# A graph layer with gathered rows: single-row loads issued from a second queue, another setup order and another tail

## The chip, the cores and the metric

One core of a Trainium2 chip. The metric is device time in microseconds, the median of several runs of the whole program. The profile is one execution of it, recorded by the hardware profiler.

## The reference

One message-passing layer over 12500 nodes and 400000 edges (the edges come sorted by destination), then a residual and a layer norm:

```python
h_s = s @ lin1_ws * a * _inv(S_IN)                       # per node: 64 scalars
h_v = jnp.einsum('nci,cd->ndi', v, lin1_wv) * a ...      # and 32 vectors of 3
hid = jax.nn.silu(edge_scalars @ fc_w1 * _inv(R))        # per edge: 64 -> 64
w = hid @ fc_w2 * _inv(FC_HID)                           # 64 -> 224 weights
es, ev = h_s[edge_src], h_v[edge_src]                    # gather, 160 floats an edge
...                                                      # products of w, es, ev and edge_attr
agg = segment_sum(mid, edge_dst)                         # back to nodes
out = gate(sc(x) + lin2(agg))                            # per node
x = _layernorm(x + out)
```

## The kernel before

**Setup.** A first block turns the node features into the table `h_table` (12500 rows of 160 floats) in memory, 4 x 128 nodes at a time, and prepares weights and index columns. SyncE's queue brings its inputs in program order, beginning with `lin1_ws` and `lin1_wv`; ScalarE's queue stores the table; VectorE builds the padded weights and the checks of the index pattern between its shares of the table.

**Tiles, quads, rounds.** The edges are 3128 tiles of 128; four tiles are a quad (782), eight quads a round (97 rounds and a rest of 6 quads). Edge tile t needs the 128 rows of `h_table` that its sources name, in one slot of the ring `rows` (16 quads deep).

**Who brings the rows.** GpSimd issues one indirect DMA per tile (`gather`, L961), in the order of the tiles. A quad's gathers wait until an earlier quad has been summed (`freed`, L965: after the first 96 quads, the quad two before). The first 8 quads are made in setup. For the quads in `FETCHED` the fourth tile is left out of GpSimd's list (`gathered`, L52): SyncE brings it, as 128 DMAs of one row each (`fetch`, L863), whose addresses it loads into registers eight at a time (L866). A tile is spread over `TRIP` = 3 rounds, then handed over by one DMA into the ring slot (`hand_over`, L871). There are 30 such tiles.

**A quad's work.** VectorE: one-hot selection, seven products of weights and rows (`all_products`, L757 to L768), the window pattern. TensorE, in order: the next quad's edge weights (`weights`, L1320), every second quad the hidden layer (`hidden`, L1312), the sums of the quad before (`combine`, L1339 and L1341), the sums of this quad's tiles (`sum_tiles`, L1328). ScalarE, in order: every second quad the hidden activation (`activate`, L1012, and the load of the next edge features, L996), the copy of the combined sums (`copy_out`, L1022, four instructions), the copy of the tile sums (`copy_tiles`, L1046), the store of the quad before (`store`, L1041), which waits until the copied sums are complete and until the store before it has landed. Once a round ScalarE loads the round's eight window bases into registers (`load_bases`, L1029).

**Nodes.** Each round finishes one block of 128 nodes: SyncE loads its sums and inputs once the first quad of a later round is stored (`node_begin`, L846), TensorE turns them (L1349, L1355) and multiplies (`node_lin`, L1364), ScalarE applies the gates (L1061 to L1063) and the square root (L1067), VectorE adds and normalises, SyncE stores (`node_store`, L828). SyncE's program runs a round as: node loads, first part of its rows, the store, second part of its rows. The last two blocks have buffers of their own (`spare`) in the ring's memory and are done behind the last quad, with `keep_warm` multiplications ahead of each (L1367).

All engines run their programs in order and meet at semaphores. The loops of rounds on TensorE, ScalarE, VectorE and GpSimd are written out; SyncE's is a loop.

Of the kernel before, what the change touches and what calls it, by code (L numbers as in the profile page):

```python
# [12 lines left out]
ds = bass.ds  # L13
# [27 lines left out]
TRIP = 3  # L41
# [3 lines left out]
def fetched_quad(k):  # L45
    return RING * (TRIP * k + 7) + RING - 1


FETCHED = [fetched_quad(k) for k in range(2 * TRIPS)]


def gathered(q):  # L52
# [107 lines left out]
def setup_block(nc, io, m):  # L160

    with ExitStack() as ctx:
# [109 lines left out]
        def _(sp):  # L272

            sp.dma_start(stage_s[:], io["lin1_ws"]).then_inc(s_lin1, 16)
            for i in range(K4):
                sp.dma_start(l1v[V * i:V * i + V, :], io["lin1_wv"]).then_inc(s_lin1, 16)

# [15 lines left out]
            for c in range(1, HCHUNKS):  # L293
                load_x(c, CB * P)
                if c == 5:
                    load_dst(0)
                if c == 7:
                    load_dst(1)
                if c == 9:
# [34 lines left out]
        def _(dve):  # L334
# [48 lines left out]
            def clear():  # L383
                nc.vector.memset(m.fc2[:], 0.0)
                nc.vector.memset(m.fc1[:], 0.0).then_inc(s_fc, 1)
                nc.vector.memset(m.w5[:], 0.0)
                then(nc.vector.memset(m.mscv[:], 0.0))
# [14 lines left out]
            def self_weights():  # L402
                dve.wait_ge(s_w, n_w)
                nc.vector.tensor_scalar(m.mscs[:], stage_sc[:], S ** -0.5, None, ALU.mult)
# [64 lines left out]
            for n, (kind, c) in enumerate(UNITS):  # L469
# [17 lines left out]
                if n == 6:  # L487
                    self_weights()
                    lin2_weights(0)
                if n == 7:  # L490
                    lin2_weights(1)
                    lin2_weights(2)
                if n == 8:
                    lin2_weights(3)
                    local_nodes(0)
                for k in range(4):
                    if k and n == 8 + 3 * k:
                        local_nodes(k)
                    if n == 9 + 3 * k:
                        extreme(2 * k, m.local[:, quarter(k)], ALU.max)  # L500
                    if n == 10 + 3 * k:
                        extreme(2 * k + 1, m.local[:, quarter(k)], ALU.min)
                if n == 20:
                    window_starts()
                if n == 21:
                    earlier_starts()
                if n == 22:
                    window_steps()
                if n == 23:
                    quad_reach()  # L510
                if n == 24:
                    extreme(8, m.off[:, 0, :], ALU.max)
                    extreme(9, m.off[:, 0, :], ALU.min)
                if n == 25:
                    extreme(10, delta, ALU.max)
                    extreme(11, delta, ALU.min)
                if n == 26:
                    orders()
                if n == 27:
# [71 lines left out]
        def _(act):  # L591
            act.dma_start(m.src[:, 0:SRC_FIRST], io["srcT"][:, 0:SRC_FIRST]).then_inc(s_src, 16)
# [46 lines left out]
def edge_block(nc, io, m):  # L639

    with ExitStack() as ctx:
# [11 lines left out]
        fidx = sb("fetch_indices", [1, P], I32)  # L653
        sel = sb("sel", [P, PRING, QT, K4, W8])
# [44 lines left out]
        fetch_idx = sem("fetch_indices_loaded")  # L699
        handed = [sem(f"handed_over{b}") for b in range(2)]  # L700
        fetch_rows = [sem(f"fetched_rows{b}") for b in range(2)]
# [10 lines left out]
        n_in = [sem(f"n_in{c}") for c in range(3)]  # L712
        n_turned = sem("n_turned")
# [81 lines left out]
        def spare_bufs(v):  # L795
# [9 lines left out]
            return psum_bufs(o, bank[:, 0:512], bank[:, 512:512 + P], bank[:, 512 + P:512 + P + 2 * SO])  # L805
# [4 lines left out]
        def _(sp):  # L810
# [6 lines left out]
            def node_inputs(k, width, bufs, c):  # L817
                nodes, r = ds(k * P, width), slice(0, width)
                sp.dma_start(bufs.xin, io["xN"][ds(k * P, P), :]).then_inc(n_in[c], 16)

            def node_load(k, width, bufs, c, free):
# [4 lines left out]
                node_inputs(k, width, bufs, c)  # L826
# [6 lines left out]
            def round_of(R, quads, loading, storing):  # L833
                node_begin(R, loading, storing)
                if quads < RING:
                    sp.wait_ge(prod_ready, SPARE_FREE)
                    sp.sem_inc(loads_seen, 1)
                    node_inputs(NBLK - 2, P, spare[0], 1)
                    node_inputs(NBLK - 1, LASTN, spare[1], 2)
# [23 lines left out]
            def fetch(b, first, last):  # L863

                for at in range(first, last, BATCH):
                    sp.load(places, fidx[0:1, at:at + BATCH])  # L866
                    for n in range(BATCH):
                        node = sp.snap(places[n], min_val=0, max_val=N - 1)
                        sp.dma_start(fetched[b][at + n:at + n + 1, :], m.h[ds(node, 1), :]).then_inc(fetch_rows[b], 16)

            def hand_over(k, b, trip):  # L871

                p = FETCHED[b] % PLACES
                sp.wait_ge(fetch_rows[b], 16 * P * (trip + 1))
                sp.sem_inc(loads_seen, 1)
# [116 lines left out]
        def _(act):  # L992
# [37 lines left out]

            def store(q, i, b, u, free):
# [21 lines left out]
            def node_copy_last(k, width, bufs):  # L1053
                act.wait_ge(n_turned, 2 * k + 2)
                nc.scalar.activation(bufs.turned[:, 4, 0:width], bufs.last[:, 0:width], ACT.Copy).then_inc(n_freed, 1)

# [12 lines left out]
            def round_of(R, quads, first, turning, gating, edges=False):  # L1069
                rest = quads < RING  # L1070
                for u in range(quads):
# [14 lines left out]
                    if rest and u == 5:  # L1086
                        node_gates(R - 2, P, late)
                    if u == 0:
                        load_bases(R, quads)
                    if edges:  # L1090
                        load_edges(u)
                    if gating and u == 6:
                        node_std(R - 3, P, main)

            with act.If(miss == 0):
# [9 lines left out]
                node_copy(NBLK - 2, P, spare[0])  # L1105
                node_copy_last(NBLK - 2, P, spare[0])
                node_gates(NBLK - 2, P, spare[0])
                node_copy(NBLK - 1, LASTN, spare[1])
                node_copy_last(NBLK - 1, LASTN, spare[1])
# [29 lines left out]
        def _(dve):  # L1139
# [9 lines left out]
            def products(I, u, tiles=QT):  # L1149
# [19 lines left out]
                if q in FETCHED:  # L1169
                    dve.wait_ge(handed[FETCHED.index(q) % 2], 16 * (FETCHED.index(q) // 2 + 1))  # L1170
                vec = rows[:, QT * p:QT * p + QT, :]
# [134 lines left out]
        def _(pe):  # L1306
# [51 lines left out]
            def node_lin(k, width, bufs):  # L1358
# [3 lines left out]
                steps += [(outs, bufs.xs[:, 0:width], m.mscs[:]), (outv, bufs.xv[:, 0:width], m.mscv[:])]  # L1362
# [4 lines left out]
            def keep_warm(times):  # L1367

                for n in range(times):
# [164 lines left out]
```

## Time and profile before

| | |
|---|---|
| median of 3 runs | 3951.13 us (3949.48 to 3951.44) |
| the profiled execution | 3948.7 us, span 3946.9 us |
| TensorE busy | 94% of the span |
| GpSimd busy | 74% |
| VectorE busy | 62% |
| ScalarE busy | 51% |
| DMA queues, share of 16 engines | GpSimd's 25.4%, ScalarE's 15.5%, SyncE's 6.5% |
| gathers by GpSimd | 3063 |
| rows by SyncE | 3840 DMAs of 640 bytes |

The busy shares say how much of the span an engine's instructions fill. Issuing a DMA, loading a register and waiting are not in them, so an engine whose program issues many DMAs can be occupied for much longer than its share says. A stretch must be cut at whole rounds if times per round are to be read from it.

### The profile page before, as it was taken

How to read it: one execution, taken by the hardware profiler on the slowest of the kernel's cores; microseconds unless marked ns; L12 is line 12 of the kernel's file. 1: busy time of each engine (PE TensorE's matmuls, PEld its weight loads, DVE VectorE, ACT ScalarE, POOL GpSimd, SP SyncE). 2: the span in 40 equal slices, each digit the busy share in tenths (PEclk: the TensorE clock that was granted, in tenths of full speed). 3: DMA queues.
4: the chain of work that ended last, by engine and by line, in shares of the span. 5: the costliest groups of instructions: out<-in, count | busy, mean ns of one | idle time of the engine just before them, and what ended most of it. 6: DMA issues, size and time to landing. Idle time of an engine off the chain costs nothing.

```text
span 3946.9 us, 76077 instructions
## 1 busy us (share of the span) xinstructions
PE 3705.6 (94%) x18692; PEld 1564.4 (40%) x18692; DVE 2440.5 (62%) x7711; ACT 2023.7 (51%) x5186; POOL 2936.1 (74%) x3119
## 2 busy tenths in 40 slices
PE   7999999999999999999999999999999999999998
PEld 5344443433333334333333333333343333333333
DVE  6666666666656666666666666666666666666665
ACT  3455555554545555555555555555555555555554
POOL 5777777777777777777777777777777777777774
PEclk8999999999999999999999999999999999999999
DMA  7644444444444444444444444444444444444443
GB/s 272 181 132 126 135 133 123 129 127 128 125 129 125 129 124 130 125 129 125 129 124 130 124 130 125 130 124 129 125 128 128 127 127 126 128 125 130 125 128 98
DMA packets 378173, 519.98 MB, mean 132 GB/s; under 512 B 71248, under 2 KB 257366, under 8 KB 377562
## 3 DMA queue, kind: packets, MB, share of 16 engines
q0 software_dynamic: 148944, 254.01, 25.4%
q10 hardware_dynamic: 164522, 180.81, 15.5%
q1 hardware_dynamic: 64224, 79.97, 6.5%
q8 instruction: 151, 2.47, 0.3%
q14 instruction: 332, 2.72, 0.2%
HBM read 431.98 MB, written 80.06 MB: 130 GB/s over the span
## 4 chain that ended last, share of the span: by engine, by line
POOL 49%; PE 19%; issue 17%; DMA 7%; DVE 5%; ACT 0%; ACTq 0%; DVEq 0%; SPq 0%
POOL rows L961 49%; PE psw L1320 6%; DMA rows<-h_table,src_cols 6%; PE pst_e L1328 5%; DVE prod L757 4%; PE psg L1341 2%; PE psg L1339 2%; PE psx L1312 2%; DMA agg_table<-aggsb 1%; DVE prod L768 1%; DVE prod L767 1%; PE psx L1364 1%; ACT aggsb L1022 0%; PE psx L1349 0%; PE psw L1364 0%
## 5 line engine op out<-in xcount | busy, mean ns | idle before, releaser
L961 POOL DMA_INDIRECT rows<-h_table,src_cols x3063 | 2895.8, 945 | 966.9 <-issue 933.0
L757 DVE TENSOR_TENSOR prod<-psw,rows 128x384 f32<-128x384 f32 (+2 forms) x3128 | 1213.1, 450 | 1396.8 <-DMA rows<-h_table,src_cols 1059.0
L1320 PE MATMUL psw<-fc,hid 128*128 128x448 f32 x3128 | 1393.3, 568 | 3.0 <-ACT hid L1012 3.0
L1022 ACT ACTIVATE aggsb<-psg 32x160 f32<-32x160 f32 x3128 | 923.4, 295 | 560.0 <-PE psg L1341 519.5
L1339 PE MATMUL psg<-tsum,shifts 128*64 128x320 f32 x3126 | 1008.8, 445 | 1.0 <-ACT tsum L1046 1.0
L1328 PE MATMUL pst_e<-prod,sel 128*32 128x448 f32 x6256 | 751.9, 552 | 199.7 <-DVE prod L768 196.4
L1341 PE MATMUL psg<-tsum,shifts 128*64 128x288 f32 x3126 | 925.7, 419 | 0.0
L1320 PEld LDWEIGHTS psw<-fc,hid 128*128 128x128 f32 x3128 | 533.0, 190 | 872.5 <-issue 861.6
L1339 PEld LDWEIGHTS psg<-tsum,shifts 128*64 128x64 f32 x3126 | 363.4, 136 | 432.2 <-issue 353.4
L1012 ACT ACTIVATE hid<-psx 128x512 f32<-128x512 f32 x391 | 233.8, 598 | 557.3 <-PE psx L1312 532.1
L1046 ACT ACTIVATE tsum<-pst_e 128x448 f32<-128x448 f32 x782 | 425.5, 544 | 147.0 <-PE pst_e L1328 129.6
L1341 PEld LDWEIGHTS psg<-tsum,shifts 128*64 128x64 f32 x3126 | 363.5, 136 | 149.3
L1312 PE MATMUL psx<-es,fc 128*128 128x512 f32 x782 | 401.2, 595 | 6.8 <-DMA es<-in_esP 3.8
L1328 PEld LDWEIGHTS pst_e<-prod,sel 128*32 128x32 f32 x6256 | 123.1, 108 | 607.3 <-DVE prod L768 448.1
L767 DVE TENSOR_TENSOR prod<-psw,rows 128x256 f32<-128x256 f32 x782 | 324.6, 415 | 0.0
L1175 DVE TENSOR_TENSOR shifts<-psd,tile_offset 128x256 f32<-128x256 f32 x782 | 324.5, 415 | 0.0
L768 DVE TENSOR_TENSOR prod<-psw,rows 128x256 f32<-128x256 f32 x782 | 324.5, 415 | 0.0
L1159 DVE TENSOR_TENSOR sel<-psd,e_cols 128x128 f32<-128x128 f32 x782 | 222.1, 284 | 13.4
L1312 PEld LDWEIGHTS psx<-es,fc 128*128 128x128 f32 x782 | 148.5, 190 | 153.9 <-issue 147.2
L1061 ACT ACTIVATE act_s<-psx,a_cols 128x64 f32<-128x64 f32 x95 | 29.9, 314 | 323.7 <-PE psx L1364 310.1
L1364 PEld LDWEIGHTS psx<-w,turned 128*128 128x128 f32 x960 | 161.8, 191 | 36.5 <-issue 36.5
L1012 ACT ACT_TABLE_LOAD x94 | 120.6, 1283 | 105.3 <-PE psw L1320 101.6
(168 smaller groups left out, 1341.8 us busy)
## 6 DMA issues: line engine op xcount, KB each, us to landing
es<-in_esP ACTq DMA_DIRECT2D x391, 256.0 KB
agg_table<-aggsb ACTq DMA_DIRECT2D x782, 80.0 KB
fetched<-h_table SPq DMA_DIRECT2D x3840, 0.6 KB
rows<-h_table,src_cols POOLq DMA_INDIRECT x3063
nag<-agg_table SPq DMA_DIRECT2D x96, 320.0 KB
nxin<-in_xN SPq DMA_DIRECT2D x96, 208.0 KB
h_table<-e_cols ACTq DMA_DIRECT2D x24, 320.0 KB, 6.1
out<-yn SPq DMA_DIRECT2D x95, 80.0 KB
```

Of the source, the lines that this page charges most:

```text
L757: return nc.vector.tensor_tensor(out, w_part, ev, ALU.mult)
L767: nc.vector.tensor_tensor(w2, w[:, :, 0:S].rearrange(halves, c=V), vec[:, :, 0:S].rearrange(halves, c=V), ALU.mult)
L768: return nc.vector.tensor_tensor(out[:, :, V * B1A:V * B1A + S], w[:, :, S + 3 * V:WN], vec[:, :, 0:S], ALU.mult)
L961: nc.gpsimd.indirect_dma_start(out=rows[:, p * QT + j, :], out_offset=None, in_=m.h, in_offset=bass.IndirectOffsetOnAxis(ap=m.src[:, t:t + ...
L1012: nc.scalar.activation(hid[:], psx[:], ACT.Silu, scale=HID ** -0.5).then_inc(hid_ready, 1)
L1022: ins = nc.scalar.activation(aggsb[r, b, :], joined(psg[r, :], k), ACT.Copy)
L1046: nc.scalar.activation(tsum[:, b, 0:PW], pst[:, 0:PW], ACT.Copy).then_inc(tsum_copied, 1)
L1312: nc.tensor.matmul(psx[:], m.fc1[:], es[:], start=True, stop=True).then_inc(hid_summed, 1)
L1320: ins = nc.tensor.matmul(psw[b][:, 2 * c:2 * c + 2, 0:WN], hid[:, at:at + P], m.fc2[:].rearrange("p (t w) -> p t w", t=2)[:, :, 0:WN], sta ...
L1328: ins = nc.tensor.matmul(pst[W * j:W * j + W, 0:PW], sel[:, q % PRING, j, :, :], prod[:, q % PRING, j, :], start=True, stop=True, tile_pos ...
L1339: nc.tensor.matmul(psg[0:2 * W, 0:2 * AW].rearrange("p (s c) -> p s c", s=2), shifts[:, q % PRING, h, 0:2, :], low, start=(h == 0), stop=( ...
L1341: ins = nc.tensor.matmul(psg[2 * W:P, 0:HIGH], shifts[:, q % PRING, h, 2:K4, :], sums[:, 0:HIGH], start=(h == 0), stop=(h == before), tile ...
```

## The change

- `TRIP` becomes 2: SyncE brings a tile in two rounds instead of three, 64 rows in each, 16 addresses to a register load; 46 tiles instead of 30.
- ScalarE brings one tile in four rounds: behind the store of each quad of rounds 3 to 94 it issues four DMAs of one row each, from 32 registers that it loads once a round. The finished tile is handed over by a DMA of its own, in the third quad of the next group's first round, for a quad one round later. 23 tiles.
- GpSimd leaves those tiles out.
- Setup: `lin1_ws` and `lin1_wv` are issued by ScalarE, ahead of its other loads; SyncE loads the destination columns two to three chunks later; VectorE's preparation steps move with them.
- Tail: no `keep_warm`; the third-last block's multiplication and gates move behind the last quad's; a spare block is turned by five transposes and one copy, and the two multiplications with its own inputs come first, into another PSUM bank.

```diff
-TRIP = 3
+TRIP = 2
 def fetched_quad(k):
-    return RING * (TRIP * k + 7) + RING - 1
+    return RING * (TRIP * k + TRIP + 4) + RING - 1
+ACT_ROWS = 4
+ACT_ROUNDS = P // (RING * ACT_ROWS)
+ACT_GROUPS = (ROUNDS - 4) // ACT_ROUNDS
+def act_quad(k):
+    return RING * (ACT_ROUNDS * (k + 1) + 4) + 3
 def gathered(q):
-    return LAST_REAL if q == QUADS - 1 else QT - (q in FETCHED)
-BATCH = 8
-FETCH_ROWS = [(0, 24, 40), (40, 64, 88), (88, 112, P)]
+    return LAST_REAL if q == QUADS - 1 else QT - (q in FETCHED or q in ACT_FETCHED)
+BATCH = 16
+FETCH_ROWS = P // TRIP
...
-            sp.dma_start(stage_s[:], io["lin1_ws"]).then_inc(s_lin1, 16)
-            for i in range(K4):
-                sp.dma_start(l1v[V * i:V * i + V, :], io["lin1_wv"]).then_inc(s_lin1, 16)
...
-                if c == 5:
+                if c == 7:
                     load_dst(0)
-                if c == 7:
+                if c == 10:
                     load_dst(1)
...
+            act.dma_start(stage_s[:], io["lin1_ws"]).then_inc(s_lin1, 16)
+            for i in range(K4):
+                act.dma_start(l1v[V * i:V * i + V, :], io["lin1_wv"]).then_inc(s_lin1, 16)
             act.dma_start(m.src[:, 0:SRC_FIRST], io["srcT"][:, 0:SRC_FIRST]).then_inc(s_src, 16)
...
-                        fetch(b, FETCH_ROWS[r][0], FETCH_ROWS[r][1])
+                        fetch(b, r, 0)
                         node_store(R - 3, P, main)
-                        fetch(b, FETCH_ROWS[r][1], FETCH_ROWS[r][2])
+                        fetch(b, r, 1)
                     hand_over(k, b, trip)
...
+            sources = [act.alloc_register(f"source{n}") for n in range(RING * ACT_ROWS)]
+            def load_indices(k):
+                act.dma_start(act_idx[k % 2][:], io["srcR"][ds(act_quad(k) * QT + QT - 1, 1), :]).then_inc(act_indexed[k % 2], 16)
+            def load_places(k, r):
+                if r == 0:
+                    act.wait_ge(act_indexed[k % 2], 16 * (k // 2 + 1))
...
+                at = RING * ACT_ROWS * r
+                act.load(sources, act_idx[k % 2][0:1, at:at + RING * ACT_ROWS])
+            def fetch_rows_of(k, r, u):
+                for n in range(ACT_ROWS * u, ACT_ROWS * u + ACT_ROWS):
+                    row = RING * ACT_ROWS * r + n
+                    node = act.snap(sources[n], min_val=0, max_val=N - 1)
+                    act.dma_start(act_rows[k % 2][row:row + 1, :], m.h[ds(node, 1), :]).then_inc(act_landed[k % 2], 16)
+            def hand_over(k):
+                act.wait_ge(act_landed[k % 2], 16 * P * (k // 2 + 1))
...
+                act.dma_start(rows[:, at, :], act_rows[k % 2][:]).then_inc(act_handed[k % 2], 16)
+            def fetching(R, u):
+                k, r = divmod(R - 3, ACT_ROUNDS)
...
+                if r == 0 and u == 2 and 1 <= k <= ACT_GROUPS:
+                    hand_over(k - 1)
...
+                if u == 0:
+                    load_places(k, r)
+                fetch_rows_of(k, r, u)
+                if r == 0 and u == 5 and k + 1 < ACT_GROUPS:
+                    load_indices(k + 1)
...
                         store(R * RING + u - 1, i - 1 + b, 1 - b, (u - 1) % RING, not first or u >= 3)
-                    if rest and u == 5:
-                        node_gates(R - 2, P, late)
                     if u == 0:
                         load_bases(R, quads)
                     if edges:
                         load_edges(u)
+                    if not rest:
+                        fetching(R, u)
                     if gating and u == 6:
                         node_std(R - 3, P, main)
...
                 combine(QUADS - 1, 1, True)
-                keep_warm(6)
-                node_turn(NBLK - 2, P, spare[0], 1, 32)
-                node_turn_last(NBLK - 2, P, spare[0])
-                node_lin(NBLK - 2, P, spare[0])
-                keep_warm(2)
-                node_turn(NBLK - 1, LASTN, spare[1], 2, 32)
-                node_turn_last(NBLK - 1, LASTN, spare[1])
-                node_lin(NBLK - 1, LASTN, spare[1])
+                node_lin(ROUNDS - 2, P, late)
+                spare_turn(0, NBLK - 2, P)
+                spare_inputs(0, P)
+                pe.wait_ge(agg_copied, QUADS)
+                spare_inputs(1, LASTN)
+                spare_sums(0, NBLK - 2, P)
+                spare_turn(1, NBLK - 1, LASTN)
+                spare_sums(1, NBLK - 1, LASTN)
```

## Rows read from the trace of the kernel before

**Rows 1.** The page: busy time by engine, then the costliest group (busy, mean ns | idle)

```profile
PE 3705.6 (94%) x18692; PEld 1564.4 (40%) x18692; DVE 2440.5 (62%) x7711; ACT 2023.7 (51%) x5186; POOL 2936.1 (74%) x3119
L961 POOL DMA_INDIRECT rows<-h_table,src_cols x3063 | 2895.8, 945 | 966.9 <-issue 933.0
```

**Rows 2.** The gathers' line: ns min/median/max, first and last start; idle before it

```profile
L961 POOL DMA_INDIRECT rows<-h_table,src_cols x3063: 942/946/1003, 84.3 to 3912.4; - x192
  issue: 933.0, 2952
```

**Rows 3.** Stretches of L768, one a quad: us, busy (count, edges counted twice), clock, DMA

```profile
0.00:196.50 196.50, 9.98 (x25) 0.95 0.71 228
196.50:3815.60 3619.10, 305.39 (x737) 1.00 0.47 127
3815.60:3946.90 131.30, 9.09 (x22) 0.97 0.39 106
236.00:531.00 295.00, 26.54 (x65) 1.00 0.48 131
1000.00:1475.00 475.00, 39.81 (x96) 0.99 0.47 127
```

**Rows 4.** Busy time of each engine in two of these stretches

```profile
236.00:531.00 295.00, 295.00 (x1497) 123.33 (x1496) 195.29 (x618) 163.51 (x417) 223.07 (x237) 1.00 0.48 131
1000.00:1475.00 475.00, 449.40 (x2250) 185.99 (x2246) 292.10 (x923) 245.68 (x626) 359.22 (x381) 0.99 0.47 127
```

**Rows 5.** SyncE in order of time, one round: start us, us, what

```profile
1258.77 0.25 SPq L859 DMA_DIRECT2D fetch_indices<-in_srcR  x1
1262.33 12.16 SPq L869 DMA_DIRECT2D fetched<-h_table  x24
1280.16 0.40 SPq L831 DMA_DIRECT2D out<-yn  x1
1281.54 7.43 SPq L869 DMA_DIRECT2D fetched<-h_table  x16
1294.80 0.36 SPq L815 DMA_DIRECT2D nag<-agg_table  x1
```

**Rows 6.** Loads of eight registers, on ScalarE and on SyncE: ns min/median/max

```profile
L1029 ACTq TENSOR_LOAD <-window_base x98: 570/1130/1402, 92.6 to 3899.7; - x98
L866 SPq TENSOR_LOAD <-fetch_indices x480: 685/784/1241, 216.2 to 3738.0; - x160
```

**Rows 7.** ScalarE in order of time, start of a round: start, us, what, idle before

```profile
420.22 1.28 ACT L1012 ACT_TABLE_LOAD   x1 [0.77 <-PE psw L1320]
421.51 0.60 ACT L1012 ACTIVATE hid<-psx 128x512 f32<-128x512 f32 x1
422.27 1.22 ACT L1022 ACTIVATE aggsb<-psg 32x160 f32<-32x160 f32 x4 [0.16 <-PE psg L1341]
423.51 0.54 ACT L1046 ACTIVATE tsum<-pst_e 128x448 f32<-128x448 f32 x1
423.81 0.57 ACTq L1041 DMA_DIRECT2D agg_table<-aggsb  x1
427.35 0.31 ACT L1061 ACTIVATE act_s<-psx,a_cols 128x64 f32<-128x64 f32 x1 [3.29 <-PE psx L1364]
```

**Rows 8.** SyncE's waits from 1000 to 1500 us: us, times, longest

```profile
SPq L830 <- DVE yn L1217: 122.2, 13, 11.7
```

**Rows 9.** SyncE in order of time, the start of setup

```profile
0.76 0.59 SPq L274 DMA_DIRECT2D stage_s<-in_lin_ws  x1
1.41 1.97 SPq L276 DMA_DIRECT2D l1v<-in_lin_wv  x4
```

**Rows 10.** The tail in order of time: SyncE's loads of sums, TensorE's warm-up

```profile
3924.24 8.46 SPq L815 DMA_DIRECT2D rows<-agg_table  x2
3927.61 2.86 PE L1370 MATMUL pst_e<-tsum,ident 128*128 128x256 f32 x12
3934.79 1.06 PE L1370 MATMUL pst_e<-tsum,ident 128*128 128x256 f32 x4
```

More of the change, by code:

```diff
@@ L386, in clear @@
                 nc.vector.memset(m.w5[:], 0.0)
+                nc.vector.memset(m.mscs[:], 0.0)
                 then(nc.vector.memset(m.mscv[:], 0.0))
@@ L712, in edge_block @@
         n_in = [sem(f"n_in{c}") for c in range(3)]
+        n_x = [sem(f"n_x{v}") for v in range(2)]
         n_turned = sem("n_turned")
@@ L861, in fetch_indices, with fetch @@
                 sp.sem_inc(loads_seen, 1)
-            def fetch(b, first, last):
-                for at in range(first, last, BATCH):
+            def fetch(b, r, half):
+                first = FETCH_ROWS * r + FETCH_ROWS // 2 * half
+                for at in range(first, first + FETCH_ROWS // 2, BATCH):
                     sp.load(places, fidx[0:1, at:at + BATCH])
@@ L1055, in node_copy_last, with spare_copy @@
                 nc.scalar.activation(bufs.turned[:, 4, 0:width], bufs.last[:, 0:width], ACT.Copy).then_inc(n_freed, 1)
+            def spare_copy(v, k, width):
+                bufs = spare[v]
+                act.wait_ge(n_turned, 2 * k + 2)
+                src = bufs.all.rearrange("p (c n) -> p c n", c=CHUNKS)[:, :, 0:width]
+                nc.scalar.activation(bufs.turned[:, :, 0:width], src, ACT.Copy).then_inc(n_freed, 2)
             def node_gates(k, width, bufs):
@@ L1365, in node_lin, with spare_inputs, spare_turn, spare_sums @@
                 ins.then_inc(n_lin, 1)
-            def keep_warm(times):
-                for n in range(times):
-                    nc.tensor.matmul(pst[:, 0:256], m.ident[:], tsum[:, 0, 0:256], start=True, stop=True)
+            def spare_inputs(v, width):
+                bufs = spare[v]
+                pe.wait_ge(n_x[v], 16)
+                nc.tensor.matmul(bufs.lin[0:width, :], bufs.xs[:, 0:width], m.mscs[:], start=True, stop=False, skip_group_check=True)
+                nc.tensor.matmul(bufs.lin[0:width, SO:2 * SO], bufs.xv[:, 0:width], m.mscv[:], start=False, stop=False,
+                                 skip_group_check=True)
+            def spare_turn(v, k, width):
+                bufs = spare[v]
+                pe.wait_ge(n_in[1 + v], 16)
+                eye = m.ident[0:width, 0:width]
+                for n in range(CHUNKS):
+                    out = bufs.four[:, P * n:P * n + width] if n < 4 else bufs.last[:, 0:width]
+                    ins = nc.tensor.matmul(out, bufs.ag[0:width, P * n:P * n + P], eye, start=True, stop=True, is_transpose=True,
+                                           skip_group_check=True)
+                ins.then_inc(n_turned, 2)
+            def spare_sums(v, k, width):
+                bufs = spare[v]
+                pe.wait_ge(n_freed, 3 * k + 2)
+                for n in range(CHUNKS):
+                    ins = nc.tensor.matmul(bufs.lin[0:width, :], bufs.turned[:, n, 0:width], m.w5[:, n, :], start=False,
+                                           stop=(n == CHUNKS - 1), skip_group_check=True)
+                ins.then_inc(n_lin, 1)
             def round_of(R, quads, first, turning, gating):
@@ L1394, in round_of @@
                     sum_tiles(q)
-                    if rest and u == 5:
-                        node_lin(R - 2, P, late)
             with pe.If(miss == 0):
```

93 lines of the change are left out of this document (56 added, 37 removed).

## The prediction

> **What bounds the kernel now.** I read the page first, then the gathers' own line, then busy time over stretches cut at whole rounds, then ScalarE and SyncE in order of time.
>
> The page makes TensorE look like the bound (94% busy) beside a GpSimd at 74% [rows 1]. The gathers' line says otherwise: 3063 gathers run from 84.3 to 3912.4 us without a pause, 0.946 us each, with some 0.3 us of issue between them [rows 2]. That is (3912.4 - 84.3) / 3062 = 1.250 us per gather, all the way. A round of 8 quads is 32 tiles, of which SyncE brings one in three rounds: 31.67 x 1.250 = 39.59 us. The stretch from 1000 to 1475 us holds 96 quads, 12 rounds, so 39.58 us each [rows 3]: GpSimd sets the pace there. From 236 to 531 us it does not: 64 quads in 295 us, 36.87 us a round, with TensorE busy for all 295 us [rows 3, 4]. So TensorE's own limit is 36.9 us a round. ScalarE is busy 163.5 / 8 = 20.4 us of a round in the one stretch and 245.7 / 12 = 20.5 in the other, whatever the pace [rows 4].
>
> **The change part by part.**
>
> Gathers. SyncE's tiles go from 30 to 46 (one in two rounds), ScalarE brings 23 (one in four): 39 gathers fewer, 3024. 39 x 1.250 = 48.8 us less on GpSimd, and its round becomes (128 - 3) / 4 x 1.250 = 39.07 us. TensorE's 36.9 is still below that, so all of it is gained if nothing else becomes slower than 39.07.
>
> ScalarE's rows. Each round adds 32 row DMAs to ScalarE's queue, one load of 32 registers, and a quarter of a hand-over and of an index load. A row costs, on SyncE now: 16 rows and one register load took 7.43 us, the load 0.78, so (7.43 - 0.78) / 16 = 0.416 us [rows 5, 6]. ScalarE issues in order: what follows the rows in the program (hidden activation, copy of the next quad's sums) can't start before the fourth row is out. So I sum what a round needs of ScalarE with no waiting at all. Busy 20.4. Store issue that the copy of the tiles doesn't cover: the copy ends at 423.51 + 0.54 = 424.05, the store at 423.81 + 0.57 = 424.38, 0.33 us, times 8 is 2.6 [rows 7]. The load of eight bases 1.13 [rows 6]. Starts: gaps between neighbours are 0.02 (copy of the sums, copy of the tiles) to 0.16 us (activation, copy of the sums) [rows 7]; fourteen in a round at 0.08 are 1.1. Together 25.2 us. The old round of 39.6 hides that: ScalarE idles 3.3 us before the gates alone [rows 7]. Added: rows 32 x 0.416 = 13.3. The load of 32 registers shows nowhere; the bounds are the shortest load of eight, 0.57, and four medians of eight, 4 x 1.13 = 4.5 [rows 6]. I take 1.3, nearer to the lower, because the same eight registers took 0.57 and 1.13, so most of a load is not paid per register. Hand-over and index load, 1 to 2 us in four rounds, 0.4. Sum: 25.2 + 13.3 + 1.3 + 0.4 = **40.2 us** a round. Its bounds: 38.0 with the load at 0.6, a row at 0.39 and starts at half, and 43.4 with the load at 4.5.
>
> That load has a rule against it. The rows show eight registers in 0.78 us on SyncE and 1.13 on ScalarE, 0.10 and 0.14 us a register. The Trainium skill, "Runtime: NRT & Kernel Launch", section "Instruction fetch mechanics", puts a register load at about 200 ns a register even in bulk; 32 would be 6.4 us, and the sum 45.3 instead of 40.2. Both rows are below that rule.
>
> 40.2 is over GpSimd's 39.07 and over the 39.34 us that these rounds take now: the rows are issued in rounds 3 to 94, 92 rounds, which the stretch from quad 24 to quad 760 covers in 3619.1 us [rows 3]. Where it shows: ScalarE is fullest around the turn of a round (two table loads, two register loads, the gates). The hidden activation of the first quad comes late, TensorE waits for it with the weights of the second quad and then for the copied tiles with the combination of sums; GpSimd, whose gathers wait until the quad two before is summed, waits in turn.
>
> SyncE. Per two rounds: 128 rows x 0.416 = 53.2, eight loads of 16 registers at 0.8 to 1.6, I take 1.0, 8; indices from 1258.77 to 1262.33, 3.6; two node loads and two stores about 4, hand-over about 3 [rows 5, 6]. That is 72 (70 to 77) of 78.1 us: hidden by the gathers, at 92%. It waits 122.2 us in 500 for the normalised rows now [rows 8], 9.7 a round; that cover goes. Queued behind the 32 rows that follow a store are the next block's loads: now issued 14.6 us after the store (1280.16 to 1294.80) [rows 5], then 32 x 0.416 + 2 + 0.7 = 16 to 19 us after it. TensorE transposes them in the sixth quad, 5 x 4.9 = 24 us into the round; landing later costs a stall of a microsecond or two in every other round, which a pace of 39 to 40 covers over 36.9.
>
> Setup. Five small loads of 0.59 + 1.97 us leave the head of SyncE's queue [rows 9], so the node features start 2.5 us earlier; ScalarE issues these five first, where it has nothing else. The sources' load behind them is later, needed only at the tenth chunk. The destinations come later, and with them VectorE's checks. I take -2.5, bounds -6 and +2.
>
> Tail. The warm-up multiplications on the path, 2.86 and 1.06 us, go [rows 10]; each spare block is turned with one copy instead of two and two multiplications of its sum come earlier. But the last block can't be turned before its sums are stored and loaded: SyncE's two loads lie 8.46 us from the first's start to the second's end [rows 10]. So little of the 4 us is kept: -2, bounds -4 and +1. The two last rounds carry no rows and may run nearer TensorE's 36.9: -3, bounds -6 and 0.
>
> Sum for 40.2: 196.5 - 2.5 + 92 x 40.2 + 131.3 - 2 - 3 = 4018.7 us of span, where 196.5 and 131.3 are what lies around the stretch [rows 3]. The profiled execution of before took 3948.7 for a span of 3946.9, and the median is 3951.1: 4.2 over the span. So **4023 us**.
>
> **The rivals.**
>
> GpSimd stays the bound (faster). Price: 3951.1 - 48.8 - 2.5 - 2 = 3898 us. For it: the gathers run without a pause now, and my sum passes 39.07 by only 1.1 us of 40. It decides where ScalarE's sum falls below 39.07; a row of 0.38 us instead of 0.416 does it, or half of the starts and the least load. Against it: the row's interval is measured, three instructions with their gaps, and every other term is a duration that stands in the trace. It holds more than a sum of small terms would give it, because a term counted twice is the likeliest fault of such a sum.
>
> The two meet: a round between 39.07 and 39.5, within 8 us of 3951. The neutral point is 39.34 + 7.5 / 92 = 39.42 us.
>
> The register load is paid per register: 4 x 1.13 = 4.5 us, a round of 43.4, 4018.7 + 92 x 3.2 + 4.2 = 4317 us. For it: loads of eight take twice a load's minimum; against it: 0.57 for the same eight. (The Trainium skill's rule named above, 6.4 us, would give 45.3 and 4492.)
>
> SyncE becomes the bound: at 1.9 us a load of 16 its two rounds are 79.2, 39.6 a round, VectorE waits for handed-over rows, about 3951 + 92 x 0.26 - 7.5, some 3970 us. Against it: 0.78 for eight.
>
> **How the numbers follow.** ScalarE the bound at about 40.2 (39.5 to 41.6, 3955 to 4150 us) 0.56; GpSimd still the bound 0.31; the two meeting 0.06; load per register 0.04; SyncE 0.03. What a measurement of this kernel can tell from no change is 0.2%, 8 us. Faster 0.31, same 0.06, slower 0.63. The likeliest case's own range is 3955 to 4150. For 8 in 10 the range has to reach to the faster case: 3893 to 4150 leaves out the load per register, a little of the faster case's low end and of the slower one's high end.
>
> **What would show it.** Right: rounds of 40 us or more between 500 and 3800 us; GpSimd waiting for the summed tiles, not for issue alone; TensorE below 94%; ScalarE's idle time nearly all behind its own issue, its copies of the sums starting just behind the fourth row. Wrong: 3024 gathers back to back at 1.250 us and VectorE waiting for rows as now. A register load near 1 us and rows near 0.4 us on ScalarE's queue confirm the terms; a row of 0.35 us or less, or copies that start while rows are being issued, would be where the forecast breaks.

## The result, and the profile after

The changed kernel takes **4143.5 us** (median of 4 runs, 4139.1 to 4149.7), the kernel before 3951.3 in the same comparison: ratio 1.0486, 95% interval 1.0472 to 1.0500. It is slower by 192 us; the forecast was 4023, slower by 72. The profiled execution took 4149.7 us, its span is 4147.9.

From the page of the changed kernel: busy time by engine, the chain that ended last by engine and by line, and the gathers' group, which answers to [rows 1].

```profile
PE 3761.1 (91%) x18676; PEld 1568.3 (38%) x18676; DVE 2432.0 (59%) x7712; ACT 1952.1 (47%) x5184; POOL 2903.2 (70%) x3080
...
ACTq 39%; ACT 23%; issue 22%; DMA 7%; PE 3%; SPq 2%; POOL 1%; DVE 0%; DVEq 0%
ACTq L1068 18%; ACT aggsb L1037 17%; ACTq L1106 10%; DMA agg_table<-aggsb 6%; ACTq L1061 4%; ACTq L1067 3%; ACT hid L1027 2%; ACTq L1044 2%; SPq L883 1%; PE psw L1392 1%; POOL rows L976 1%; ACT L1027 1%; DMA nxin<-in_xN 1%; ACT vec_s L1134 1%; ACT turned L1120 1%
...
L976 POOL DMA_INDIRECT rows<-h_table,src_cols x3024 | 2862.9, 947 | 1206.3 <-issue 900.8
```

Every engine's share fell, ScalarE's too (51% to 47%), though ScalarE now sets the time: the chain runs through its queue (ACTq) and its instructions for 62% of the span, and the largest line of it is L1068, the new row DMAs. GpSimd, once the whole pace, is 1% of it.

The stretches that answer to [rows 3], cut at the same quads by the last product of a quad (L781: 782 of them, one a quad). Columns: stretch, us, VectorE's busy time (count), granted clock, DMA share, GB/s.

```profile
0.00:192.50 192.50, 10.29 (x25) 0.95 0.71 231
192.50:4026.50 3834.00, 301.90 (x735) 0.99 0.45 122
4026.50:4147.90 121.40, 9.03 (x22) 0.98 0.42 114
1000.00:1500.00 500.00, 39.42 (x96) 1.00 0.45 122
```

96 quads, 12 rounds, now take 500 us: **41.7 us a round**, where before had 39.58 [rows 3]. TensorE's granted clock is 1.00 in this stretch, so the clock doesn't explain it. By the starts of the products of quads 24 and 760 (192.0 and 4026.8 us) the 92 rounds with rows take 3834.8 us, 41.68 each. The 201 us between the two profiled executions are: these rounds +215.7 (3834.8 against 3619.1), what lies ahead of them -4.4, what lies behind -10.2.

The gathers' line, which answers to [rows 2]: what ended its idle time (us, times).

```profile
L976 POOL DMA_INDIRECT rows<-h_table,src_cols x3024: 941/947/973, 83.7 to 4118.9; - x189
...
  issue: 900.8, 2846
  PE pst_e L1400: 305.5, 178
```

The second of these rows in the kernel before, then TensorE's weight loads waiting for ScalarE in the changed kernel (us, times, longest):

```profile
  PE pst_e L1328: 33.8, 111
...
PEld psw L1392 <- ACT hid L1027: 526.9, 374, 3.0
PEld psg L1411 <- ACT tsum L1111: 410.9, 470, 1.8
```

There are 3024 gathers, as counted, and they no longer run without a pause: GpSimd waits 178 times for the sums of the tiles of an earlier quad, 305.5 us in all (once for 35.9 us, from 519 us on, where `freed` begins to ask for the quad two before). Before, 33.8 us stood there, at most 0.3 at a time. TensorE in turn waits for ScalarE's hidden activation and copied tiles, 526.9 and 410.9 us; before these were 10.9 and 69.7. That is the chain that the prediction described.

ScalarE in order of time, as in [rows 7], in two places of one round: a plain quad, then the turn of the round.

```profile
1512.04 1.20 ACT L1037 ACTIVATE aggsb<-psg 32x160 f32<-32x160 f32 x4
1513.26 0.54 ACT L1111 ACTIVATE tsum<-pst_e 128x448 f32<-128x448 f32 x1
1513.58 0.58 ACTq L1106 DMA_DIRECT2D agg_table<-aggsb  x1
1514.32 1.51 ACTq L1068 DMA_DIRECT2D act_rows<-h_table  x4
1515.94 0.60 ACT L1027 ACTIVATE hid<-psx 128x512 f32<-128x512 f32 x1 [2.14 <-issue]
...
1516.44 1.21 ACT L1037 ACTIVATE aggsb<-psg 32x160 f32<-32x160 f32 x4
...
1528.78 0.54 ACT L1111 ACTIVATE tsum<-pst_e 128x448 f32<-128x448 f32 x1
1529.08 0.58 ACTq L1106 DMA_DIRECT2D agg_table<-aggsb  x1
1533.17 1.67 ACTq L1068 DMA_DIRECT2D act_rows<-h_table  x4
1534.96 0.31 ACT L1132 ACTIVATE act_s<-psx,a_cols 128x64 f32<-128x64 f32 x1 [5.65 <-issue]
```

The brackets are to be read first. They say "issue": ScalarE's next computing instruction waited for no other engine, only for its own queue to get through the store and the rows. In the plain quad that is 1515.94 - 1514.16 = 1.78 us for four rows, 0.445 each. At the turn 3.5 us lie between the end of the store (1529.66) and the first row (1533.17): the two register loads. Such a bracket holds all the idle time of the computing instructions and names what ended it; the queue may have been issuing for part of it. Before, 3.29 us stood ahead of the gates at this place [rows 7], and of these 1.7 were a wait for TensorE, the rest the store and the load of bases; now all 5.65 us are ScalarE's own issue.

The durations of ScalarE's queue instructions, each from its own line: ns min/median/max, then first and last start.

```profile
L1068 ACTq DMA_DIRECT2D act_rows<-h_table x2944: 227/234/578, 201.8 to 4027.5; - x197
...
L1061 ACTq TENSOR_LOAD <-act_indices x92: 1954/1970/1986, 199.6 to 3990.3; - x92
...
L1044 ACTq TENSOR_LOAD <-window_base x98: 567/1144/1371, 92.0 to 4105.4; - x98
...
L880 SPq TENSOR_LOAD <-fetch_indices x368: 1136/1232/1821, 214.3 to 4033.7; - x184
```

I gave each nanosecond of ScalarE from 1000 to 3400 us to a computing instruction, else to the queue instruction being issued or the gap ahead of it. Per round: computing 19.66 us, rows 13.96 (0.436 each, gaps and address included), stores not covered 2.94, the load of 32 registers 1.95, the load of bases 1.15, hand-over and index load 0.22, all the rest 1.8. Of this rest 0.97 are gaps just ahead of a computing instruction, 0.24 are waits for an earlier store to land, and the others are semaphore and register instructions of the queue with their gaps. These make 41.7, with practically nothing idle.

SyncE's waits for others from 1000 to 1500 us, which answer to [rows 8]: us, times, longest.

```profile
SPq L843 <- DVE yn L1289: 24.5, 6, 7.4
SPq L874 <- DMA fetch_indices<-in_srcR: 16.3, 6, 3.4
SPq L890 <- DMA fetched<-h_table: 13.5, 6, 2.4
```

Of the 122.2 us that it waited for VectorE's rows before [rows 8], 24.5 are left. Over 1000 to 3400 us it waits for other engines 133 us in all, 2.3 a round; the other 39.4 us are its own program with the landings that it waits for itself.

### The profile page after: what moved, and what is told of

It reads as the page before. It is cut to its first block, busy times and chain, and to the rows that moved or that the text cites. A ratio compares the mean times of both kernels' runs of the same rounds, so it can differ in the third digit from the quotient of the medians.

```text
span 4147.9 us, 91412 instructions
## 1 busy us (share of the span) xinstructions
PE 3761.1 (91%) x18676; PEld 1568.3 (38%) x18676; DVE 2432.0 (59%) x7712; ACT 1952.1 (47%) x5184; POOL 2903.2 (70%) x3080
## 4 chain that ended last, share of the span: by engine, by line
ACTq 39%; ACT 23%; issue 22%; DMA 7%; PE 3%; SPq 2%; POOL 1%; DVE 0%; DVEq 0%
ACTq L1068 18%; ACT aggsb L1037 17%; ACTq L1106 10%; DMA agg_table<-aggsb 6%; ACTq L1061 4%; ACTq L1067 3%; ACT hid L1027 2%; ACTq L1044 2%; SPq L883 1%; PE psw L1392 1%; POOL rows L976 1%; ACT L1027 1%; DMA nxin<-in_xN 1%; ACT vec_s L1134 1%; ACT turned L1120 1%
## 5 line engine op out<-in xcount | busy, mean ns | idle before, releaser
L976 POOL DMA_INDIRECT rows<-h_table,src_cols x3024 | 2862.9, 947 | 1206.3 <-issue 900.8
L1392 PE MATMUL psw<-fc,hid 128*128 128x448 f32 x3128 | 1412.1, 575 | 234.3 <-ACT hid L1027 232.7
L1411 PEld LDWEIGHTS psg<-tsum,shifts 128*64 128x64 f32 x3126 | 363.7, 136 | 524.5 <-ACT tsum L1111 410.9
L781 DVE TENSOR_TENSOR prod<-psw,rows 128x256 f32<-128x256 f32 x782 | 321.2, 411 | 0.0
L1287 DVE RECIPROCAL rstd<-rstd 128x1 f32<-128x1 f32 x95 | 15.5, 163 | 456.2 <-ACT rstd L1138 456.2
L1229 DVE TENSOR_TENSOR sel<-psd,e_cols 128x128 f32<-128x128 f32 x782 | 220.3, 282 | 13.3
```

Source lines behind the costliest of these rows:

```text
L976: nc.gpsimd.indirect_dma_start(out=rows[:, p * QT + j, :], out_offset=None, in_=m.h, in_offset=bass.IndirectOffsetOnAxis(ap=m.src[:, t:t + ...
L1392: ins = nc.tensor.matmul(psw[b][:, 2 * c:2 * c + 2, 0:WN], hid[:, at:at + P], m.fc2[:].rearrange("p (t w) -> p t w", t=2)[:, :, 0:WN], sta ...
L1411: nc.tensor.matmul(psg[0:2 * W, 0:2 * AW].rearrange("p (s c) -> p s c", s=2), shifts[:, q % PRING, h, 0:2, :], low, start=(h == 0), stop=( ...
```

## The experiments

Each kernel is the changed one with the edit shown; each was compared with the kernel before on the same chip (3947.5, 3947.5 and 3948.5 us in the three comparisons).

**1. No rows on ScalarE.** SyncE's new schedule, setup and tail stay; GpSimd gathers the 23 tiles.

```diff
-ACT_FETCHED = [act_quad(k) for k in range(ACT_GROUPS)]
+ACT_FETCHED = []
...
-                    if not rest:
-                        fetching(R, u)
```

> The changed kernel without ScalarE's rows; GpSimd brings those 23 tiles again. Theory (ScalarE's in-order issue is the bound of the changed kernel, 41.7 us a round): the round falls to GpSimd's (128 - 2) / 4 x 1.25 = 39.4 us, with SyncE, which is occupied for 39.3 us of each round of the changed kernel, close behind; 4143.5 - 92 x 2.3 = about 3932 us. Rival (SyncE's two-round tiles or the traffic of the many small DMAs make the loss): SyncE's part stays, over 4050 us.

Measured: 3928.1 us (3924.5 to 3930.1), ratio 0.9951 (0.9935 to 0.9968). So ScalarE's part costs 4143.5 - 3928.1 = 215 us between the medians, and the rest of the change gains 19; by the two comparisons, each with its own run of the kernel before, the part costs 192 + 19 = 212. The rival is out. The gathers run without long pauses again, (3893.6 - 82.0) / 3046 = 1.251 us each:

```profile
L975 POOL DMA_INDIRECT rows<-h_table,src_cols x3047: 940/946/987, 82.0 to 3893.6; - x191
```

**2. The rows issued, but their result not used.** The finished tile goes to a buffer that nobody reads, and GpSimd gathers these tiles as well.

```diff
-    return LAST_REAL if q == QUADS - 1 else QT - (q in FETCHED or q in ACT_FETCHED)
+    return LAST_REAL if q == QUADS - 1 else QT - (q in FETCHED)
...
-                act.dma_start(rows[:, at, :], act_rows[k % 2][:]).then_inc(act_handed[k % 2], 16)
+                act.dma_start(act_sink[:], act_rows[k % 2][:]).then_inc(act_handed[k % 2], 16)
...
-                if q in ACT_FETCHED:
-                    dve.wait_ge(act_handed[ACT_FETCHED.index(q) % 2], 16 * (ACT_FETCHED.index(q) // 2 + 1))
```

> ScalarE issues all its rows as in the changed kernel, but its tiles go to a buffer that nobody reads, and GpSimd gathers these 23 tiles too. Theory (ScalarE is the bound by 2.3 us a round): GpSimd's 23 more gathers, 39.4 us a round, are hidden; 4143 us, within 10. Rival (the gathers that are left out still count): 4143.5 + 23 x 1.25 = 4172 us.

Measured: 4139.7 us (4138.8 to 4143.7). 23 more gathers cost GpSimd 29 us and the kernel nothing, and nobody waits for these tiles: it is the issuing that costs, not late tiles, and GpSimd has room to spare. The rows' traffic is still there in this run; experiments 8 and 9 keep the same 2944 rows, change only when and behind which loads they are issued, and move the time by hundreds of us, so traffic alone doesn't set it.

**3. Setup and tail alone**, with the fetching of before.

```diff
-TRIP = 2
+TRIP = 3
...
-BATCH = 16
-FETCH_ROWS = P // TRIP
+BATCH = 8
+FETCH_ROWS = [(0, 24, 40), (40, 64, 88), (88, 112, P)]
...
```

(and no rows on ScalarE, as in 1; the lines that index `FETCH_ROWS` are those of before)

> The kernel before with the new order of setup and the new tail alone: SyncE's tiles in three rounds, no rows on ScalarE. Theory: GpSimd is the bound from round 12, so only its earlier start counts, 0.8 us in the trace of the changed kernel, and the tail, 4.3 us shorter from the last products to the end: 3951.3 - 5.1 = 3946 us. Rival (the quads that run 4.4 us earlier at round 3 keep their lead): 3951.3 - 8.7 = 3943 us.

Measured: 3941.1 us (3938.7 to 3944.2), ratio 0.9982 (0.9972 to 0.9991): a gain of 6.5 us, between the theory's 5.1 and the rival's 8.7. The time alone doesn't choose; the trace does. Its gathers' line is beside [rows 2] the same stream, begun earlier:

```profile
L974 POOL DMA_INDIRECT rows<-h_table,src_cols x3063: 942/946/972, 83.2 to 3911.3; - x192
```

3828.1 us from first to last start, as before. So setup is worth only the 1.1 us by which GpSimd begins earlier, although quad 24 is reached 3.2 us earlier (193.3 against 196.5 us): that lead is used up while GpSimd bounds, and 1.1 us of it is left at quad 760 (3814.5 against 3815.6). From the last quad's products to the end it takes 22.2 us instead of 26.1.

**4. Two rows behind each store**, so one tile in eight rounds.

```diff
-ACT_ROWS = 4
+ACT_ROWS = 2
```

> ScalarE issues two rows per quad instead of four (a tile in eight rounds, 11 tiles, a register load of 16). Theory: ScalarE's round is 41.7 - 16 x 0.436 - 0.8 = 33.9 us and no bound; GpSimd's (256 - 5) / 8 x 1.25 = 39.2, SyncE's 39.3; about 4143.5 - 92 x 2.4 = 3923 us. Rival (what costs is having another chain in ScalarE's queue at all: hand-over, register load and its waits, not the rows): about half of the loss stays, some 4050 us.

Measured: 3947.3 us (3935.2 to 3960.6 in 10 runs), ratio 1.0004 (0.9991 to 1.0016). Neither number: 200 us of loss are gone with half the rows, so cost isn't in proportion to rows, but 24 us of what I expected is missing. SyncE's waits from 1000 to 3400 us in the profiled run:

```profile
SPq L874 <- DMA fetch_indices<-in_srcR: 88.1, 30, 4.4
SPq L890 <- DMA fetched<-h_table: 59.2, 30, 2.4
SPq L843 <- DVE yn L1289: 9.8, 12, 1.3
```

SyncE waits for another engine 9.8 us in 2400, for its own DMAs 147. It issues 64 rows in 39.3 us, all of its round. That makes a new theory: SyncE is the next bound. This trace can't prove it, since GpSimd's own round, 39.2 us, is hardly shorter.

**5. Two rows, and SyncE's loads twice as long**, half as many. BATCH concerns SyncE alone.

```diff
-ACT_ROWS = 4
+ACT_ROWS = 2
...
-BATCH = 16
+BATCH = 32
```

> Two rows behind each store in place of four, and SyncE loads its row numbers 32 at a time in place of 16. The run with two rows alone took 3947 us, where the gathers left to GpSimd would have given some 3910 (3036 x 1.2502 us, begun at 82 and followed by a tail of 29); in it SyncE waited for nothing but its own loads and landings, 64 rows in 39.3 us. Theory (SyncE's issue was the bound there): two loads of some 2.0 us in place of four of 1.25 take 1.1 us off SyncE's round, to 38.2, GpSimd bounds again: 3912 us (3904 to 3925). Rival (ScalarE's sixteen rows delay the sums' copies and so hold the round): unchanged, 3947 us within 10.

Measured: 3917.3 us (3910.9 to 3918.9), ratio 0.9920 (0.9906 to 0.9934): inside the theory's range (3904 to 3925), and the best of all kernels here. SyncE's wait for VectorE from 1000 to 3400 us, then its loads and the gathers, by line:

```profile
SPq L843 <- DVE yn L1289: 61.0, 31, 5.1
```

```profile
L880 SPq TENSOR_LOAD <-fetch_indices x184: 2030/2154/2900, 211.6 to 3789.7; - x184
...
L976 POOL DMA_INDIRECT rows<-h_table,src_cols x3036: 942/947/974, 82.0 to 3887.9; - x190
...
  PE pst_e L1400: 16.5, 30
```

Waiting for VectorE rose from 9.8 to 61.0 us, GpSimd's pauses fell from 37.1 us to 16.5, and the gathers run at (3887.9 - 82.0) / 3035 = 1.254 us: GpSimd bounds again. One line that only SyncE's program reads gave 30 us between the medians, so SyncE's issue was in the way, and SyncE's own work is now 38.2 us a round, as expected. The two profiled executions lie 17 us apart. In them rounds 27 to 93 take 39.36 and 39.28 us; most of the difference arises in the rounds before, where GpSimd's gathers don't yet set the pace.

**6. Four rows, with the long loads on SyncE.**

```diff
-BATCH = 16
+BATCH = 32
```

> The changed kernel, four rows behind each store, with SyncE loading its row numbers 32 at a time in place of 16: SyncE's round, 39.3 us of work in 41.7, becomes 1.1 us shorter, ScalarE's is untouched. Theory (ScalarE alone sets the round): 4140 us (4130 to 4150). Rival (SyncE, some 95% full, shares in setting the round): most of 1.1 us a round comes off, 4040 to 4100 us.

Measured: 4136.5 us (4133.2 to 4138.8). The same line that gave 30 us with two rows gives at most 7 with four: there ScalarE alone sets the round.

**7. No rows on ScalarE, with the long loads on SyncE.**

```diff
-ACT_FETCHED = [act_quad(k) for k in range(ACT_GROUPS)]
+ACT_FETCHED = []
...
-BATCH = 16
+BATCH = 32
```

> No rows on ScalarE (as in the run without them, 3928 us, where GpSimd makes 3047 gathers), and SyncE loads its row numbers 32 at a time. It asks whether the 11 tiles that two rows a store bring (3917 us with the long loads, 3036 gathers) are worth anything. Theory (with SyncE 0.8 us a round shorter GpSimd bounds both, at 1.2502 us a gather): 11 gathers more than the version with two rows, 14 us longer less the pauses that GpSimd had there (some 9 us): 3923 us (3917 to 3929). Rival (ScalarE's rows cost as much as they save): 3915 us or less.

Measured: 3923.2 us (3919.6 to 3923.4), ratio 0.9936 (0.9922 to 0.9950). As expected. The 11 tiles that two rows a store bring (experiment 5) are worth about 6 us between the medians; the intervals of the two ratios overlap and the two ran on different chips, so the sign is likely, the size is not settled.

**8. The load of 32 registers cut into eight of 4**, one ahead of each quad's rows.

```diff
-                at = RING * ACT_ROWS * r
-                act.load(sources, act_idx[k % 2][0:1, at:at + RING * ACT_ROWS])
...
+                at = RING * ACT_ROWS * r + ACT_ROWS * u
+                act.load(sources[ACT_ROWS * u:ACT_ROWS * u + ACT_ROWS], act_idx[k % 2][0:1, at:at + ACT_ROWS])
```

> The changed kernel with ScalarE's one load of 32 registers a round cut into eight loads of 4, one ahead of the rows of each quad; rows, hand-overs and all else stay. By the loads read so far (one register 0.485 us, eight 0.78, sixteen 1.23, thirty-two 1.97, so some 0.485 + 0.048 for each further register) eight loads of 4 take 8 x 0.63 = 5.0 us a round where one load took 1.97: 3.1 us more. Theory (ScalarE has no idle time, every microsecond of its issue lengthens the round): 92 x 3.1 = 280 us more, 4424 us (4390 to 4450). Rival (the loads lie in time in which ScalarE waits anyway, the round is set elsewhere): 4143 us, within 30.

Measured: 4723.6 us (4719.7 to 4730.7): 580 us more, where I expected 280. A load hidden in waiting time is out. The size of the load was wrong:

```profile
L1064 ACTq TENSOR_LOAD <-act_indices x736: 310/867/1482, 198.9 to 4604.8; - x184
```

Four registers take 0.87 us, not 0.63. In the order of the quads, the first load of a round takes 0.314 us on the mean, each of the other seven 0.87 to 0.92: together 6.6 us a round against 1.97. Rounds 24 to 89 take 48.0 us each, 6.3 longer; the loads' 4.6 are most of it, row DMAs that take 0.291 us on the mean instead of 0.265 are 0.8, waiting ahead of the gates 0.6, and the rest is in other gaps. TensorE's granted clock was lower in this run (0.956 against 0.988); whether the 0.6 us, a wait for TensorE, come from that is not shown.

**9. The same 32 rows in the four middle quads**, eight behind each store, none around the turn of the round.

```diff
-                for n in range(ACT_ROWS * u, ACT_ROWS * u + ACT_ROWS):
+                if not 2 <= u < 6:
+                    return
+                for n in range(2 * ACT_ROWS * (u - 2), 2 * ACT_ROWS * (u - 1)):
```

> The changed kernel with ScalarE's 32 rows of a round in its four middle quads, eight behind the store of each, and none in the four quads around the turn of the round, where ScalarE also makes the hidden activations, the gates and the normalising of a node block. Theory (it is the sum of ScalarE's work over a whole round, 41.7 us, that counts): unchanged, 4140 us (4120 to 4165). Rival (only the turn of the round is too full, and rows there are what delays TensorE): some 1 us a round or more is given back, below 4060 us.

Measured: 4383.3 us (4373.8 to 4400.2), slower by another 240 us. Both were wrong: the rival in the sign, and my sum because it held for ScalarE's whole round, which this edit leaves as it was. ScalarE in order of time, one round, first the copies of the tile sums, one a quad, with two places at which it waits, then the rows:

```profile
1502.50 0.54 ACT L1113 ACTIVATE tsum<-pst_e 128x448 f32<-128x448 f32 x1
...
1507.17 0.54 ACT L1113 ACTIVATE tsum<-pst_e 128x448 f32<-128x448 f32 x1
...
1511.36 0.31 ACT L1134 ACTIVATE act_s<-psx,a_cols 128x64 f32<-128x64 f32 x1 [3.64 <-PE psx L1438]
...
1513.38 0.54 ACT L1113 ACTIVATE tsum<-pst_e 128x448 f32<-128x448 f32 x1
...
1515.57 0.60 ACT L1027 ACTIVATE hid<-psx 128x512 f32<-128x512 f32 x1 [1.65 <-PE psx L1386]
...
1518.05 0.55 ACT L1113 ACTIVATE tsum<-pst_e 128x448 f32<-128x448 f32 x1
...
1519.10 3.15 ACTq L1070 DMA_DIRECT2D act_rows<-h_table  x8
...
1523.60 0.54 ACT L1113 ACTIVATE tsum<-pst_e 128x448 f32<-128x448 f32 x1
...
1524.66 3.07 ACTq L1070 DMA_DIRECT2D act_rows<-h_table  x8
...
1529.56 0.54 ACT L1113 ACTIVATE tsum<-pst_e 128x448 f32<-128x448 f32 x1
```

A quad with eight rows takes 5.96 us (1523.60 to 1529.56), and ScalarE's gaps there are its own issue. The quad with the gates takes 6.21; the bracket of 3.64 us names TensorE, but the two register loads fill it (1508.06 to 1511.21), so this quad too is ScalarE's own. The quad behind it takes 4.67, and there ScalarE does wait for TensorE: most of the 1.65 us, and again ahead of the copy.

On the mean of 66 rounds (24 to 89), from one copy of the tile sums to the next:

| kernel | first quad to eighth, us | round |
|---|---|---|
| changed | 7.96, 4.49, 4.19, 4.80, 4.51, 4.55, 5.44, 5.74 | 41.7 |
| this experiment | 6.23, 4.65, 5.81, 6.07, 5.99, 6.15, 4.75, 4.61 | 44.3 |

The four quads that got more rows grow by 6.0 us, the four that lost theirs give back only 3.4. The waits explain it: in three of the relieved quads (second, seventh, eighth) ScalarE now stands idle for 0.5 to 1.4 us, where the changed kernel has almost no such wait. What ScalarE has left in one quad doesn't carry over to the next: the round is the sum of the later of the two, quad by quad. TensorE's granted clock was lower in this run (0.961 against 0.988), in each round 3.4 us at the lower of its two levels (1.2 GHz), most of it in the seventh quad. But the four relieved quads together take 20.2 us, no more than the same four in the kernel before (20.5), so the clock can explain little of the 2.6 us.

## Why the prediction went as it did

**Right: the sign, the bound and where it shows.** Rounds of 40 us or more between 500 and 3800 us (41.7), GpSimd waiting for summed tiles (305.5 us), TensorE below 94% (91%), ScalarE's gaps put down to its own issue: all four signs came, and experiments 1, 2 and 8 show that the issue of the rows is the cause. The sign that was to confirm the terms came by half: rows near 0.4 us, but a register load of 1.97 us, not near 1. That GpSimd's relief (39 gathers, 48.8 us) is worth nothing while ScalarE bounds was the step that decided the sign, and experiment 2 measures it for 23 of them. The rival with GpSimd as the bound, at 0.31, would have needed a sum 1.1 us smaller; it is 2.6 us over 39.07. One thing was luck: the prediction summed ScalarE's work over a whole round and didn't ask whether an empty quad can make up for a full one. Here the rows are spread evenly and every quad is full, so the sum held; experiment 9 shows 2.6 us a round by which it fails when they are not.

**Wrong: the size of ScalarE's sum, 40.2 us a round; it is 41.7.** 1.48 x 92 = 136 us, less 7 that setup and tail gained beyond my terms, are the 129 us by which the span misses. The forecast loss was a small difference of two large numbers, 40.2 less the 39.34 of before, so 1.5 us too little in the sum (4%) made the loss of these rounds 79 us instead of 216. The step that failed is the pricing of four terms: the rows, the load of 32 registers, the stores and the rest around them, 2.35 us too little together. By terms, forecast and measured:

| term, us a round | forecast | measured |
|---|---|---|
| computing | 20.4 | 19.66 |
| 32 rows | 13.3 | 13.96 |
| load of 32 registers | 1.3 | 1.95 |
| stores not covered | 2.6 | 2.94 |
| load of bases | 1.13 | 1.15 |
| hand-over and index load | 0.4 | 0.22 |
| starts and the rest | 1.1 | 1.8 |

No one term is out by more than 0.75 us, but five of the seven miss to the same side. Computing is less because instructions that stand ready behind one another overlap (the copy at 1516.44 begins 0.10 us before the activation of 1515.94 ends; in [rows 7] 0.16 us lie between the two; the durations add up to 20.8 us a round before and 20.7 now); that and the hand-over give back 0.9 of the 2.4 that the others add. The starts themselves were about right, 0.97 us against 1.1; what the sum left out is the queue's semaphore and register instructions and the waits for landed stores. Two terms rest on a reading that failed.

The rows: 0.416 us was one batch of 16 on SyncE; on ScalarE a row takes 0.436, on the mean from 1000 to 3400 us.

The load: I argued from "the same eight registers took 0.57 and 1.13" that most of a load isn't paid per register. It is the other way round. Loads of 4 (experiment 8), 16 (experiments 4 and 5) and 32 behind another load on ScalarE take 0.314, 1.024 and 1.970 us: 0.08 + 0.059 for each register, which gives 0.55 for eight, near the 0.57 of [rows 6]. That 0.57 was a single load, the first of the 98, begun 0.58 us after the queue's last instruction; the other 97 begin 0.03 us behind a store's DMA, take 1.08 us or more, and so pay 0.5 to 0.6 us more ahead of the same registers. Had I read the 0.57 as the price of eight registers, 32 would have been some 2 us. The upper bound, 4.5, multiplied the start as well. One more reading was too simple, though it enters no term: the 3.3 us of idle time ahead of the gates held only 1.7 us of waiting.

The Trainium skill, "Runtime: NRT & Kernel Launch", section "Instruction fetch mechanics", puts a register load at about 200 ns a register even in bulk. The page says it of loads that the runtime inserts; the loads here read a row that lies in on-chip memory. For them the trace doesn't agree at 32 registers (1970 / 32 = 62 ns); for 4 registers behind a DMA 870 / 4 = 217 ns would look like it, but most of that is the start.

**SyncE: hidden, but not at 92%.** I estimated 72 us (70 to 77) of two rounds; 2 x 39.4 = 78.8 are measured, beyond my range and beyond GpSimd's 78.1. The rows took 0.432 us each over the stretch, not 0.416 (2.0 us more in two rounds), the loads of 16 with their gaps 1.31, not 1.0 (2.5 more); its own landings were priced about right. Most of the rest is a term that the sum left out: the turn of SyncE's loop, once in four rounds, where 2.7 to 3.8 us lie between the branch and the next instruction (3.3 on the mean of 21 turns), 1.9 us in two rounds with the loop's own instructions. ScalarE's longer round hid this, and so the error cost nothing here; experiments 4 and 5 show it as the next bound. The rival that named it priced it at some 3970 us from loads of 1.9 us; with loads of 1.23 SyncE gets there by the sum of small terms.

**Setup and tail.** Setup: -2.5 forecast, -4.4 at quad 24, and experiment 3 shows that it counts only while GpSimd isn't the bound. Behind the last row-carrying round: -2 and -3 forecast, -10.2 measured. The two rounds without rows take 37.8 and 37.6 us, against 40.1 and 41.6 before: 6.3 us of it. From the last quad's products to the end it takes 21.8 us instead of 26.1: 4.3. I had argued that the loads of the sums stay on the path and left 2. They do stay, but they begin 2.0 us after the last quad's products (4128.11) and take 7.10 us, where before they began 3.4 us after them (3924.24) and took 8.46 [rows 10].

**Open.** Why the ten runs with two rows (experiment 4) spread over 25 us, and the four of experiment 9 over 26, where those of the other kernels lie within some 11: the trace of each is of its fastest run, so it can't show what holds the slower ones. And why an empty quad can't make up for a full one: that the buffers between the engines are only one or two quads deep is a likely reason, but no run changes their depth.

## What to carry to other kernels

An engine that looks half idle by its busy share may have no time to issue DMAs: sum what a period needs of its queue with every instruction, DMA, register load and wait, and if the sum comes within a tenth of the period, take the upper side of each small term. Do it step by step as well as for the whole period, since a full step may not be able to borrow from an empty one (experiment 9); the sum over the period is only a floor. And when one bound is lifted, work out the next queue's sum with the same care: here SyncE's 39.4 us lay above GpSimd's 39.07 already.

## What the runs showed of the hardware that I had not expected

- **Loads into registers are paid per register, behind a start that depends on what went ahead.** On ScalarE behind another load: 0.314, 1.024 and 1.970 us for 4, 16 and 32 registers, 59 ns each and 0.08 us of start. On ScalarE behind a store: 0.89 us for 4 and 1.144 for 8, some 0.65 us of start; the first load of 8, 0.58 us after the last instruction before it, took 0.567. On SyncE, behind rows: 0.784, 1.232 and 2.154 us for 8, 16 and 32, 57 ns each and some 0.32 us of start. What the start is, no run here tells.
- **A DMA of one row occupies the issuing queue for 0.43 to 0.44 us** on either engine, of which the DMA instruction itself is 0.234 (median); the rest is the address's move, its arithmetic and the gaps. Where loads are mixed in between (experiment 8) the instruction's mean rises from 0.265 to 0.291.
- **A turn of SyncE's loop left its queue idle for 2.7 to 3.8 us** (changed kernel, 21 turns from 1000 to 3400 us), between the branch at the loop's end and the next instruction. What fills that time, no run here tells.
